# A chain of four layers: six blocks' transposes moved from TensorE to VectorE and DMA, and the third matmul stage one step later

## The reference

```python
x = x + L0(x)     # temporal layer: causal averages, gates, four products, layer norm of the result
x = x + L1(x)     # x @ W[cat] + b[cat]                                  (512x512)
x = x + L2(x)     # h = relu(x @ W1[lang] + b1); x2 = x + h @ W2[lang] + b2
                  # L2 = (x2 - mean) * rsqrt(var + 1e-5) * gamma[lang] + beta[lang]
x = x + L3(x)     # x @ weight[subj].T + bias[subj]                      (512x512)
```

## Time and profile before

| | us |
|---|---|
| median of 3 runs (lowest, highest) | 757.25 (757.16, 759.28) |
| the profiled execution | 757.63 |
| its span, first to last instruction | 755.7 |
| TensorE busy | 743.7 |
| VectorE busy | 535.2 |
| ScalarE busy | 367.0 |
| GpSimd busy | 119.4 |

### The profile page before, as it was taken

One profiled execution on the slowest core, in us unless ns is written; L12 is line 12 of the kernel. 1 busy time (PEld: TensorE's weight loads), 2 busy tenths in 40 slices (PEclk: granted clock), 3 DMA queues, 4 the chain that ended last, 5 costly groups with the idle time before them and its releaser, 6 DMA issues.

```text
span 755.7 us, 10450 instructions
## 1 busy us (share of the span) xinstructions
PE 743.7 (98%) x3421; PEld 605.6 (80%) x3421; DVE 535.2 (71%) x782; ACT 367.0 (49%) x550; POOL 119.4 (16%) x226
## 2 busy tenths in 40 slices
PE   7999999999999999999999998999999999999997
PEld 6888888888888888888888786888888888888885
DVE  4598895695695595596597589666877767667645
ACT  5363346445435535535545632756564553636331
POOL 2000040030022013004004046115201021010110
PEclk9999999999999999999999999999999999999999
DMA  9973007926925953962962863426143131322002
GB/s 256 232 181 43 28 1 115 186 62 101 191 70 84 186 92 71 179 111 56 181 124 46 142 202 111 168 84 210 56 167 122 72 126 47 135 98 83 28 33 81
DMA packets 93020, 86.17 MB, mean 114 GB/s; under 512 B 61583, under 2 KB 75950, under 8 KB 90942
## 3 DMA queue, kind: packets, MB, share of 16 engines
q1 hardware_dynamic: 91614, 81.57, 45.7%
q10 hardware_dynamic: 1184, 4.23, 1.8%
q0 software_dynamic: 192, 0.00, 0.1%
HBM read 33.33 MB, written 25.20 MB: 77 GB/s over the span
## 4 chain that ended last, share of the span: by engine, by line
PE 95%; DVE 2%; POOL 1%; ACT 1%; issue 1%; DMA 0%; DVEq 0%; ACTq 0%
PE pc L612 12%; PE pc L614 12%; PE pc L613 12%; PE pm L612 6%; PE pm L613 6%; PE pm L614 6%; PE pt L614 6%; PE pt L612 6%; PE pt L613 6%; PE pm L727 4%; PE pm L729 4%; PE pm L728 4%; PE pm L619 3%; PE pt L619 3%; PE pm L861 1%; PE pm L862 1%
## 5 line engine op out<-in xcount | busy, mean ns | idle before, releaser
L612 PE MATMUL pc<-x_h,wg_h 128*128 128x512 f32 x224 | 88.7, 396 | 0.0
L614 PE MATMUL pc<-x_h,wg_l 128*128 128x512 f32 x224 | 87.9, 393 | 0.0
L613 PE MATMUL pc<-x_l,wg_h 128*128 128x512 f32 x224 | 87.7, 391 | 0.0
L1424 DVE TENSOR_TENSOR_SCAN stage_b<-alpha,carry,stage_b 128x512 f32<-128x512 f32 x64 | 80.3, 1297 | 0.0
L727 PE MATMUL pm<-t_h,wt_h 128*128 128x512 f32 x128 | 50.5, 395 | 2.9 <-ACT stage_a L1115 2.9
L612 PE MATMUL pm<-wo_h,s_h 128*128 128x512 f32 x128 | 50.7, 396 | 0.0
L614 PE MATMUL pm<-wo_h,s_l 128*128 128x512 f32 x128 | 50.5, 395 | 0.0
L613 PE MATMUL pm<-wo_l,s_h 128*128 128x512 f32 x128 | 50.5, 395 | 0.0
L729 PE MATMUL pm<-t_h,wt_l 128*128 128x512 f32 x128 | 50.5, 394 | 0.0
L728 PE MATMUL pm<-t_l,wt_h 128*128 128x512 f32 x128 | 50.4, 393 | 0.0
L612 PEld LDWEIGHTS pc<-x_h,wg_h 128*128 128x128 f32 x224 | 42.1, 188 | 10.2 <-issue 1.0
(11 more groups left out here) (245 smaller groups left out, 1919.1 us busy)
## 6 DMA issues: line engine op xcount, KB each, us to landing
x_planes<-x_pairs SPq DMA_DIRECT2D x52, 256.0 KB, 7.4
xt_scratch<-x_t SPq DMA_DIRECT2D x8, 1024.0 KB, 10.3
n_scratch<-stage_a SPq DMA_DIRECT2D x8, 1024.0 KB, 10.1
ctx_t<-xt_scratch SPq DMA_DIRECT2D x16, 512.0 KB, 6.6
x_pairs<-n_scratch SPq DMA_DIRECT2D x14, 512.0 KB, 5.7
out_dram<-x_tok SPq DMA_DIRECT2D x28, 256.0 KB, 2.0
mod<-mod_scratch ACTq DMA_DIRECT2D x8, 512.0 KB, 3.7
stage_b<-in_L_cond_weight_dram SPq DMA_DIRECT2D x2, 1024.0 KB, 5.4
```

The costliest lines, as they stand in the source:

```text
L612: nc.tensor.matmul(acc, ah, bh, start=start and q == 0, stop=False)
L613: nc.tensor.matmul(acc, ah, bl, start=False, stop=False)
L614: last = nc.tensor.matmul(acc, al, bh, start=False, stop=stop and q == n - 1)
L1424: nc.vector.tensor_tensor_scan(tr[:, m % 2, :], alpha[:, 1 + d:2 + d].to_broadcast([P, BLK]), tr[:, m % 2, :], carry[:, D - d, m:m + 1], A ...
```

## The change

For blocks 1 to 6 TensorE no longer turns n2. ScalarE normalises all four tiles in the next step; VectorE transposes each tile in squares of 32x32 into `stage_b` (`turn_squares`); SyncE moves the squares to their partitions in `x_planes` with 16 DMAs of 64 KB (`move_n2`, SBUF to SBUF, pieces of 512 bytes); ScalarE multiplies by gamma and adds beta (`scale_n2`), back into `stage_b`; VectorE adds x2 there. L3 of a block therefore runs one step later (block i-2 in step i), and x2 of two blocks is alive, so it lies in `x_t` and `soma` in turn. `x2_beta` is gone. Blocks 0 and 7 are turned by TensorE as before, with beta added in `x3_hi_part` and `x3_lo_part`. The adapter's second raw weights go to `gate`, and are prepared in step 3. The low parts of the second L3 weights use pc0 and pc1 only. All loops of the second half are written out. Step 1 runs two tiles of block 0's L3 and step 2 the other two; behind step 7 come L3 of block 6, the transposes of block 7 between its tiles 1 and 2, and L3 of block 7.

```diff
+        def x2_of(i):
+            return x_t if i % 2 == 0 else soma
+        def x3_parts_of(j):
+            return (s_h, s_l) if j == LAST - 1 else (t_h, t_l)
+        squares = stage_b[:, :, :].rearrange("p a e -> p (a e)").rearrange("p (f k i) -> p f k i", k=TILES, i=32)
+        squares_q = stage_b[:, :, :].rearrange("p a e -> p (a e)").rearrange("p (c q r) -> p c q r", c=NC, q=4)
...
+            def move_n2(j):
+                sp.wait_ge(n2_squares, j * TILES)
...
+                for q in range(4):
+                    for a in range(4):
+                        part, tok = slice(32 * a, 32 * a + 32), slice(P * a, P * a + P)
+                        sp.dma_start(x_planes[32 * q:32 * q + 32, :, tok],
+                                     squares_q[part, :, q, :]).then_inc(n2_in, 16)
...
+            for i in range(2, NBLK):
+                move_n2(i - 1)
...
+                store_out(i - 2, 0)
+                store_out(i - 2, 1)
+                if i + 2 < NBLK:
+                    load_y(i + 2)
+                store_out(i - 2, 2)
+                store_out(i - 2, 3)
...
+            def l3_tile(j, k):        # PE; waits
...
+                    after(pe, out_ready, j * TILES + max(k - 1, 0))
...
+            def second_step2():
+                for m in range(NC):
+                    if m < 2:
+                        pe.wait_ge(l3_hi, 2 * NC)
+                        pe.wait_ge(l3_lo, 2 * NC)
+                    l1_product(2, 0, m)
+                l3_tile(0, 2)
+                w1_product(2, 0)
+                l3_tile(0, 3)
+                for k in range(TILES):
+                    xx_product(2, 0, k)
+
+            def step2(i):
+                b = i // PER_SEQ
+                l1_product(i, b, 0)
+                l1_product(i, b, 1)
+                if turns_y(i):
                     turn_y(i + 1, 0)
                     turn_y(i + 1, 1)
+                l1_product(i, b, 2)
+                l1_product(i, b, 3)
+                if turns_y(i):
                     turn_y(i + 1, 2)
                     turn_y(i + 1, 3)
+                l3_tile(i - 2, 0)
+                w1_product(i, b)
+                l3_tile(i - 2, 1)
+                l3_tile(i - 2, 2)
                 for k in range(TILES):
                     xx_product(i, b, k)
+                l3_tile(i - 2, 3)
+
+            def last_blocks():
+                l3_tile(LAST - 1, 0)
+                l3_tile(LAST - 1, 1)
+                turn_n2(LAST)
+                l3_tile(LAST - 1, 2)
+                l3_tile(LAST - 1, 3)
...
+            def scale_n2(j, m):       # ACT
...
+                act.wait_ge(n2_in, j * 256)
+                nc.scalar.activation(stage_b[:, m, :].rearrange("p (k a i) -> p k a i", k=TILES, a=4),
+                                     x_planes[:, m, :].rearrange("p (a k i) -> p k a i", k=TILES, a=4), ACT.Identity,
+                                     bias=seq["beta_b2"][:, b, m:m + 1],
+                                     scale=seq["gamma2"][:, b, m:m + 1]).then_inc(n2_scaled, 1)
...
+            def step2(i):             # ACT
+                if i >= 3:
+                    for m in range(NC):
+                        x3_hi_part(i - 2, m)
+                normalise(i - 1, 0)
+                normalise(i - 1, 1)
+                x2_parts(i, 0)
+                normalise(i - 1, 2)
+                normalise(i - 1, 3)
+                x2_parts(i, 1)
+                if i == PER_SEQ - 1:
                     adapter_hi(1)
+                x2_parts(i, 2)
+                if i < LAST:
                     y_hi_part(i + 1, 0)
                     y_hi_part(i + 1, 1)
+                x2_parts(i, 3)
+                if i < LAST:
                     y_hi_part(i + 1, 2)
                     y_hi_part(i + 1, 3)
+                relu_part(i)
+                for m in range(NC):
+                    scale_n2(i - 1, m)
...
+            def turn_squares(j, k):   # DVE
+                dve.wait_ge(n2_act, n2_acts(j - 1) + k + 1)
...
+                nc.vector.transpose(squares[:, :, k, :], stage_a[:, k, :].rearrange("p (f i) -> p f i", i=32)
+                                    ).then_inc(n2_squares, 1)
+
+            def step2(i):             # DVE
+                j = i - 2
+                if j >= 1:
+                    for m in range(NC):
+                        x3_lo_part(j, m)
+                turn_squares(i - 1, 0)
+                turn_squares(i - 1, 1)
+                x2_lo_part(i, 0)
+                turn_squares(i - 1, 2)
+                turn_squares(i - 1, 3)
+                x2_lo_part(i, 1)
...
+                output(j, 2 if j == 0 else 0)
...
+                hid_lo_part(i)
+                x3_sum_part(i - 1, 0)
+                x3_sum_part(i - 1, 1)
+                output(j, 3 if j == 0 else 1)
+                x3_sum_part(i - 1, 2)
+                x3_sum_part(i - 1, 3)
+                if i == LAST:
+                    for m in range(NC):
+                        x3_lo_part(LAST - 1, m)
+                if j > 0:
+                    output(j, 2)
                 for k in range(TILES):
                     norm2_stats(i, k)
+                if j > 0:
+                    output(j, 3)
```

More of the change, by code:

```diff
@@ L855, in xx_product @@
                     pe.wait_ge(hid_lo, i + 1)
-                if k < (2 if last_block(i) else 3):
-                    after(pe, out_ready, i * TILES + (k - 3))
+                    if i >= 2:
+                        pe.wait_ge(n2_act, n2_acts(i - 1))
+                if k < 3 and i >= 2 and turns_y(i):
+                    pe.wait_ge(out_ready, (i - 2) * TILES + k + 1)
                 tok = out_cols(k)
-                turn(pm[k], [x_t[:, c, tok] for c in range(NC)], stop=False)
+                turn(pm[k], [x2_of(i)[:, c, tok] for c in range(NC)], stop=False)
@@ L864, in xx_product @@
+                nc.tensor.matmul(pm[k][:, :], hl, wh, start=False, stop=False, skip_group_check=True)
+                nc.tensor.matmul(pm[k][:, :], hh, wl, start=False, stop=True,
                                  skip_group_check=True).then_inc(xx_mm, 1)
[L866 to L876, removed]
-                    turn(n2_bank(j, c), [stage_a[:, k, out_cols(c)] for k in range(TILES)]).then_inc(tn_done, 1)
@@ L879, in l3_product, with turn_n2 @@
[L879 to L887, removed]
+            def turn_n2(j):
+                pe.wait_ge(n2_act, n2_acts(j))
+                pe.wait_ge(n2_dve, 2 if j == 0 else 4)
+                for c in range(NC):
+                    turn(n2_bank(j, c), [stage_a[:, k, out_cols(c)] for k in range(TILES)]).then_inc(tn_done, 1)
@@ L901, in step2 @@
[L901 to L918, removed]
+                ch, cl = x3_parts_of(j)
@@ new lines, in _ @@
+            x3_sum_part(0, 3)
+            x3_lo_part(0, 2)
+            x3_lo_part(0, 3)
+            hid_lo_part(1)
+            y_sum_part(2, 0)
+            y_sum_part(2, 1)
+            output(0, 0)
+            y_sum_part(2, 2)
+            y_sum_part(2, 3)
+            y_lo_part(2, 0)
+            y_lo_part(2, 1)
+            output(0, 1)
+            subject_lo(1, 0, pc[0])
+            subject_lo(1, 1, pc[1])
+            y_lo_part(2, 2)
+            y_lo_part(2, 3)
+            for k in range(TILES):
+                norm2_stats(1, k)
@@ L1740, in _ @@
+            subject_lo(1, 2, pc[0])
+            subject_lo(1, 3, pc[1])
+            for i in range(2, NBLK):
+                step2(i)
+            normalise(LAST, 2)
+            normalise(LAST, 3)
+            output(LAST - 1, 0)
+            output(LAST - 1, 1)
+            x3_sum_part(LAST, 0)
+            x3_sum_part(LAST, 1)
             x3_lo_part(LAST, 0)
-            x3_sum_part(LAST, 1, 2)
+            x3_sum_part(LAST, 2)
             x3_lo_part(LAST, 1)
-            x3_sum_part(LAST, 1, 3)
+            x3_sum_part(LAST, 3)
```

459 lines of the change are left out of this document (205 added, 254 removed).

## The result

The median of 7 runs is 763.54 us (761.80 to 766.97) against 759.00 (757.16 to 760.64) in 7 runs of the kernel before: ratio 1.0068, 95% interval 1.0052 to 1.0084. That is 4.5 us slower; the forecast was 755.6. The profiled execution took 766.97, span 765.2.

The account below looks back on a forecast made before the run. TensorE, busy 98% of the span, was taken to set the time. Removed work of 11.7 + 1.3 = 13.0 us less 11.3 of new waits made it 1.7 us faster: median 755.6, own range 754 to 757.5.

Parts of the forecast that it names:

- (a): Start of step 2: TensorE waits before L1 of block 2 for VectorE's low parts of L3 weights, 4.6 us.
- (b): Step 3: wait before L1 chunk 2, from a later Newton chain (2.9) and VectorE contention (1.3), 4.2 us together.
- (c): Step 4: GpSimd's low parts of the second adapter weights meet x3_lo, 1.2 us with the plain wait.
- (d): Step 7: the plain step's wait of TensorE, 0.35 us.
- (e): Tail: L3 tile 0 of block 6 waits for output 3 of block 5, 1.0 us.
- The waits at the edges: Step of the prediction adding new TensorE waits at the start of step 2, in steps 3, 4, 7 and the tail: 11.3 us.
- (5): Rival: an unseen wait of one or two us a step, 759 to 763 us; chance 0.08.
- The 14 switches: TensorE's changes from transposes to matmuls that go away, 0.085 us each, claimed to save 1.2 us.
- Rival (2): VectorE's square transpose costs what a scan costs, 1.30 us, giving 762.4 us; chance 0.12.
- rival (1): The n2 transfer decides: 19 us gives 776 us, some 3.4 us per us beyond 13.1; chance 0.10.
- rival (3): VectorE and GpSimd contention in steps 3 and 4 (1.3 and 0.85 us) stays out, 753.4 us; chance 0.25.
- Rival (4): No new wait shows on TensorE, 744.3 us; chance 0.03.

Follow-up runs that it names:

- fill_two: The changed kernel with twelve throw-away matmuls in each of TensorE's two long waits, before L1 of block 2 and before L1 chunk 2 of block 3: 759.74 us.
- rest_14: The kernel before, with TensorE made to wait ahead of W1 in steps 2 to 6 for 14 tiny GpSimd operations, waits of 3.3 to 3.8 us: 788.12 us.
- rest_28: The kernel before, with TensorE made to wait ahead of W1 in steps 2 to 6 for 28 tiny GpSimd operations, waits of 5.4 to 5.8 us: 797.39 us.
- fill_two_queues: fill_two with 8 of each block's 16 n2 transfers issued by GpSimd's queue instead of SyncE's: 758.66 us, ratio 0.9996.
- filled_queues: fill_two_queues with nine throw-away matmuls also put into the first half's wait: 758.66 us, ratio 0.9987.
- after_warm: The changed kernel with its three long waits filled and twelve throw-away transposes ahead of the first real one, transfers on one queue: 758.24 us, ratio 0.9996.
- moves_32: The changed kernel with each block's n2 moved by 32 transfers of 32 KB instead of 16 of 64 KB: 821.20 us.
- pause_6: The kernel before, with TensorE meant to wait ahead of W1 in steps 2 to 6 for six GpSimd operations, though nothing waited: 759.16 us.
- pause_3: The kernel before, with TensorE meant to wait ahead of W1 in steps 2 to 6 for three GpSimd operations, though nothing waited: 758.85 us.
- tiles_apart: The changed kernel with block 0's L3 tile 2 moved ahead of L1 of block 2 and tile 3 behind XX of block 2: 770.29 us, ratio 1.0148.

## Why the prediction was wrong

- **The waits**, counted as the forecast did, from where the next matmul would have started: (a) 4.3 us (forecast 4.6), (b) 4.25 (4.2), (c) 1.2 (1.2), (d) 0.4 (0.35), (e) 0.9 (1.0). The trace's idle times are 0.17 less each. Right. One more was not forecast: 0.55 us in step 1 (at 536.01), for VectorE's low part of block 0's x3. Together 11.6 against 11.3.
- **What a wait costs.** The failed step is "The waits at the edges": it priced a wait at its length. A wait of about 4 us costs some 2.1 us more behind it, 1.6 and 2.5 here, because the clock has gone to its lower level (fill_two against the change, rest_14 and rest_28). None of my rivals had it. The nearest, (5), gave 759 to 763, but a wait and not a clock.
- **What is removed.** 96 transposes at 0.109 were right: steps 5 and 6 went from 33.05 to 31.29. That is 1.76, 16 x 0.109 and no more. The 14 switches at 0.085 had been counted twice: in the earlier trace rows the transposes take 0.79 from 581.71 to 582.50, and the 0.87 that I divided by eight has the 0.085 in it. 1.2 us too much. The turned step came out at 31.29, not 31.05.
- **The sum.** -1.7, plus 1.2 for the switches, 0.3 for the waits and 4.1 of clock is 3.9, against the 3.8 between the two profiles from step 1 on. Without the clock the same sum is -0.2, and with the waits filled and the transfers on two queues the profiles have -0.5 and -0.6 (fill_two_queues, filled_queues). With one queue step 3's wait is 1.3 longer: 1.1, measured 0.7 (after_warm). So no term of the size of the clock is missing, and what is left open is 0.4 us. The difference of the medians is 4.5; the start and the first half are in it too.
- **The square transpose** took 0.69 us a 128x512 (695 ns over 24), the value taken. Rival (2) falls.
- **The transfer**, rival (1). It took 12 to 13 us rather than 11. In the changed kernel the lost clock of TensorE covered it, but for 1.25 us in step 4, and no wait of TensorE follows that one. With the clock repaired it was last on ScalarE in three or four steps and cost TensorE 1.3 us. It was no rival to the forecast but part of it. My 0.41 for an issue came from the wrong row; the 0.65 of the spreads was nearer.
- **Contention**: rival (3), that it stays out, falls. In step 3 it had its forecast size, 1.3. In step 4 the adapter's low parts took 3.20 us instead of the 2.58 of the earlier trace rows. Rival (4), no new wait, is excluded by (a).
- **Slips in the working.** A transfer of 15.2 us gives by the slope 755.6 + 2.1 x 3.4 = 762.7, not 770. In the plain step x2's pair ends at S+5.05, not 4.95. Neither touches the forecast by more than 0.05 us.
- The plain step's wait, squares, and tail order behaved as written (step 7: 30.1 us with a wait of 0.4); the x2 buffers, the written-out loops and the stores are behind none of TensorE's six waits.

What stays open is which of two equal waits is followed by the low clock, and for how long. Ten of the profiles have the first half's wait unfilled. In four of them the low clock followed (waits of 3.2, 2.9, 2.5 and 2.4 us: after, fill_two, moves_32, pause_6), in six it did not (2.9, 2.9, 2.7, 2.7, 2.6, 2.4 us: before, pause_3, rest_14, tiles_apart, fill_two_queues, rest_28). And wait (a), 4.10 us in the changed kernel and in moves_32 alike, cost 1.6 us of clock in the one and 2.6 in the other.

## What to carry to other kernels

Price a wait of TensorE, where it sets the time, at its length plus what its clock loses behind it (1.6 to 2.6 us here for every wait of 3.3 us or more that the experiments set), and look at the granted clock, not at the busy share, which stays full. Waits of up to 1.5 us that stood alone showed none of it here, and those of 2.4 to 3.2 us in some runs only; where one of 3 or 4 can't be avoided, work whose result is thrown away is worth putting in. When a stage is made quicker, ask which transfer had been covered by its slowness, and count the issues on its queue before its bytes. When a group's hold is divided by its members, check that its edge isn't priced a second time.

## What was not expected of the hardware

- The lower clock behind waits of 3.3 to 5.8 us: ten times of ten, 2.1 us each in the mean, whatever the wait's length within that. Behind a wait of 2.4 us it came in one profile (pause_6) and not in another (rest_28).
- TensorE's first microseconds run at one of two speeds from run to run (16 transposes in 1.9 us, or in 2.8 to 3.6), with the granted clock shown as 1.00 in both; with twelve transposes ahead of the first load it was the quick one in four profiles of four.
- TensorE's queue sends a semaphore increment that stands alone ahead of the matmuls before it: in pause_6 GpSimd began to answer one 3.5 us before the matmul behind it started.
- 32 KB and 64 KB transfers inside SBUF both take 0.60 us to issue on SyncE's queue, and 0.55 on GpSimd's.
